# LoRA B on the halves of the array: a four-layer conditional kernel on one core

## The reference

```python
def lora_add(base, inp, A, B):
    Ab = A[layer_idx][lora_indices]
    Bb = B[layer_idx][lora_indices]
    t = jnp.einsum('bri,bni->bnr', Ab, inp)
    return base + jnp.einsum('bor,bnr->bno', Bb, t) * SCALE       # SCALE 0.5, rank 16
gate = lora_add(jnp.einsum('bnh,fh->bnf', x, W_gate), x, A_gate, B_gate)
up = lora_add(jnp.einsum('bnh,fh->bnf', x, W_up), x, A_up, B_up)  # f: 1376 columns
act = jax.nn.silu(gate) * up
down = lora_add(jnp.einsum('bnf,hf->bnh', act, W_down), act, A_down, B_down)
```

## Time and profile before

| | us |
|---|---|
| median of 3 runs | 1031.28 |
| lowest and highest | 1030.27, 1031.84 |
| the profiled execution | 1029.79 |
| its span | 1028.0 |
| TensorE busy in the span | 1001.4 |
| VectorE, GpSimd, ScalarE busy | 762.1, 486.6, 421.7 |
| from one tile's first product to the next tile's | 28.29 |

### The profile page before, as it was taken

How to read it: one execution, slowest core, us unless ns; L and a number is a source line. 1 busy time by engine, 2 the same in 40 slices (tenths; PEclk the granted TensorE clock), 3 DMA queues, 4 the chain that set the end, 5 groups by cost and what they waited for, 6 DMA issues and landing times.

```text
span 1028.0 us, 19764 instructions
## 1 busy us (share of the span) xinstructions
PE 1001.4 (97%) x5668; PEld 882.1 (86%) x5668; DVE 762.1 (74%) x2087; ACT 421.7 (41%) x660; POOL 486.6 (47%) x301
## 2 busy tenths in 40 slices
PE   2999999999999999999999999999999999999998
PEld 2666788989899899889898989998898889899987
DVE  8343387777787788777778877887777788778864
ACT  7103244344444344443444443444434444434431
POOL 0703554555544445445555444454455554454541
PEclk9999999999999999999999999999999999999999
DMA  9899543424333333435243333334352433333320
GB/s 330 309 349 336 180 114 96 140 89 131 114 112 109 105 110 102 119 95 147 81 133 112 110 109 107 105 105 121 94 146 83 132 113 108 110 107 102 112 74 21
DMA packets 101125, 135.50 MB, mean 132 GB/s; under 512 B 26411, under 2 KB 59692, under 8 KB 101100
## 3 DMA queue, kind: packets, MB, share of 16 engines
q1 hardware_dynamic: 100524, 135.12, 43.2%
q10 hardware_dynamic: 576, 0.08, 0.0%
HBM read 118.11 MB, written 16.99 MB: 131 GB/s over the span
## 4 chain that ended last, share of the span: by engine, by line
PE 91%; DMA 3%; DVE 3%; SPq 2%; issue 1%; ACT 0%; DVEq 0%; ACTq 0%
PE ps L1032 48%; PE ps L1064 27%; PE ps L1042 8%; PE ps L1010 3%; DMA x1p<-yo 1%; DMA tr<-kpad 1%; PE ps L1053 1%; PE ps L1087 1%; PE ps L1086 1%; PE ps L1023 1%; PE ps L1021 1%; PE ps L1020 1%; SPq L212 1%; SPq L279 0%; DVE xs L735 0%
## 5 line engine op out<-in xcount | busy, mean ns | idle before, releaser
L484 POOL TENSOR_TENSOR bst<-braw,bst 128x1024 fp32r<-128x1024 f32 (+1 forms) x96 | 212.8, 2217 | 313.5 <-ACT bst L591 313.5
L843 DVE STREAM_TRANSPOSE ps<-act_t 32x128 f32<-32x128 f32 x1008 | 325.3, 323 | 14.9
L1032 PE MATMUL ps<-wg_hi,x_hi 128*128 128x512 f32 (+2 forms) x768 | 292.8, 381 | 0.2 <-DVE x_lo L836 0.2
L1032 PE MATMUL ps<-wg_lo,x_hi 128*128 128x512 f32 (+2 forms) x768 | 290.2, 378 | 0.0
L1032 PE MATMUL ps<-wg_hi,x_lo 128*128 128x512 f32 (+2 forms) x768 | 289.8, 377 | 0.0
L613 ACT ACTIVATE at_hi<-ps 128x512 fp32r<-128x512 f32 (+1 forms) x95 | 53.5, 563 | 333.6 <-DVE ps L843 275.6
L843 DVE STREAM_TRANSPOSE ps<-x3m 32x128 f32<-32x128 f32 x496 | 160.0, 323 | 9.8 <-ACT x3m L558 1.2
L1032 PEld LDWEIGHTS ps<-wg_hi,x_lo 128*128 128x128 f32 x768 | 144.3, 188 | 24.9
L1032 PEld LDWEIGHTS ps<-wg_hi,x_hi 128*128 128x128 f32 x768 | 144.4, 188 | 23.0 <-issue 0.4
L1032 PEld LDWEIGHTS ps<-wg_lo,x_hi 128*128 128x128 f32 x768 | 144.4, 188 | 22.6
L1064 PE MATMUL ps<-wd_lo,at_hi 128*128 128x288 f32 x696 | 148.9, 296 | 0.0
(11 more groups left out here) (157 smaller groups left out, 1109.5 us busy)
## 6 DMA issues: line engine op xcount, KB each, us to landing
braw<-in_tb SPq DMA_DIRECT2D x256, 128.0 KB, 2.7
braw<-in_tb SPq DMA_DIRECT2D x128, 96.0 KB, 2.4
adraw<-in_tad SPq DMA_DIRECT2D x128, 88.0 KB, 1.9
tr<-kpad SPq DMA_DIRECT2D x16, 512.0 KB, 6.7
x1p<-yo SPq DMA_DIRECT2D x16, 512.0 KB, 5.1
xb<-in_x SPq DMA_DIRECT2D x32, 256.0 KB, 2.9
agraw<-in_ta SPq DMA_DIRECT2D x128, 64.0 KB, 1.9
bdraw<-in_tbd SPq DMA_DIRECT2D x128, 64.0 KB, 2.2
```

The costliest lines, as they stand in the source:

```text
L484: sub(v, b_from(p, q), v.bitcast(F32), ALU.subtract).then_inc(s["blo"], 1)
L843: last = V.transpose(to[cols].rearrange("f (k n) -> f k n", n=P)[:, :, rows], of[rows].rearrange("n (k f) -> n k f", f=P)[:, :, cols])
L1032: last = mm(bank[:, 0:n], x3s[a][:, k, :], wgs[b][:, k, o:o + n], start=(k == 0 and a + b == 0), stop=False, skip_group_check=True)
```

## The change

The two copies of a rank value no longer lie in neighbouring rows but in halves: rows 0 to 63 and rows 64 to 127, and within a half the sequence changes fastest. In gate's columns of `bst` the lower half of the rows (0 to 63) holds B's hi and the upper its lo; in up's it is the other way round (`half` takes the place of `odd`, so `b_high` is two instructions, one for gate and one for up). The products with t_hi use all 128 rows as before. The products with t_lo use only the half that holds B's hi: rows 0 to 63 for gate, rows 64 to 127 for up.

The rank values take another way: `t_pick` copies for each sequence only its own 16 values of gate and up, twice, times 0.5 (four instructions on 32 rows x 64 columns); they are turned and split at 128x64, and four DMAs issued by ScalarE (`t_scatter`) write them from SBUF to the rows and columns of `tsc` where they belong. The rest of `tsc` is zeroed once. TensorE waits for these DMAs (`tsc`) in the place of t_low.

Also, the order of the work in a tile changes on three engines. TensorE: mix comes between the two parts of chunk 0; down of the tile before moves ahead of the first lora_b; a_turn moves behind chunk 1 up and lora_b_down. VectorE: t_low ahead of a_low, x3_turn in one piece, and act_mul of chunk 0 behind td_turn, a_low of chunk 0 behind out_sum. ScalarE: x3_copy ahead of t_high, td_high ahead of ag_high, silu of chunk 1 ahead of b_high of chunk 2, ad_high ahead of x3_keep.

```diff
@@ load_b (SyncE)
-                    sp.dma_start(brs[(p + q) % 2][b * 2 * RANK:(b + 1) * 2 * RANK, 0:w],
-                                 rows.unsqueeze(1).to_broadcast([RANK, 2, w])).then_inc(s[f"b{(p + q) % 2}"], 16)
+                    sp.dma_start(brs[(p + q) % 2][b:P:GB, 0:w],
+                                 rows.unsqueeze(0).to_broadcast([2, RANK, w])).then_inc(s[f"b{(p + q) % 2}"], 16)
@@ GpSimd, once
+            pool.wait_ge(s["y"], C)
+            pool.wait_ge(s["yst0"], 16 * C // 4)
+            pool.wait_ge(s["yst1"], 16 * C // 4)
+            nc.gpsimd.memset(tsc[:].bitcast(F32), 0.0).then_inc(s["wz"], 1)
@@ b_high, t_high, t_scatter (ScalarE)
-                copy(b_view(p, q), b_from(p, q), ACT.Copy, scale=odd[:, 0:1]).then_inc(s["bhi"], 1)
+                for u in range(2):
+                    last = copy(b_view(p, q)[:, :, u], b_from(p, q)[:, :, u], ACT.Copy, scale=half[:, u:u + 1])
+                last.then_inc(s["bhi"], 1)
...
-                copy(ts2[0][:], tr2[:], ACT.Copy).then_inc(s["thi2"], 1)
+                copy(tcs[:, 0], trc[:], ACT.Copy).then_inc(s["thi2"], 1)
+
+            def t_scatter(t):
+                act.wait_ge(s["tlo2"], t + 1)
+                for b in range(GB):
+                    cols = slice(b * C, (b + 1) * C)
+                    act.dma_start(tsc[b:P:GB, :, :, cols].bitcast(F32), tcs[cols].bitcast(F32)).then_inc(s["tsc"], 16)
@@ tile_act
                 t_high(t)
-                if not last:
-                    x3_copy(t + 1)
                 b_high(t, p, 1, None if first else t * 3)
+                t_scatter(t)
                 silu(t, p, 0)
@@ VectorE
-            def t_mask(t, p):
+            def t_pick(t, p):
                 dve.wait_ge(s["la"], t + 1)
...
+                for b in range(GB):
+                    rows = slice(b * C, (b + 1) * C)
+                    of = gub[2 * (p % 2)][rows, FW[0]:FW[0] + NAG].rearrange("p (u b r) -> p u b r", u=2, b=GB)
+                    last = V.tensor_scalar(tmc[rows], of[:, :, b].unsqueeze(2).to_broadcast([C, 2, 2, RANK]), 0.5, None,
+                                           ALU.mult)
+                last.then_inc(s["tm"], 1)
@@ lora_b (TensorE)
-                    for a in range(2):
-                        last = mm(gub[2 * ((p + q) % 2) + u][:, 0:w], ts2[a][:, u, :],
-                                  bst[:, (p + q) % 2, u * n:u * n + w], start=False, stop=(a == 1),
-                                  skip_group_check=True)
+                    mm(gub[2 * ((p + q) % 2) + u][:, 0:w], tsc[:, 0, u, :], bst[:, (p + q) % 2, u * n:u * n + w],
+                       start=False, stop=False, skip_group_check=True)
+                for u in range(2):
+                    rows = slice(u * P // 2, (u + 1) * P // 2)
+                    last = mm(gub[2 * ((p + q) % 2) + u][:, 0:w], tsc[rows, 1, u, :],
+                              bst[rows, (p + q) % 2, u * n:u * n + w], start=False, stop=True, skip_group_check=True)
@@ tile_pe
                 chunk(p, 0, 0).then_inc(s["la"], 1)
+                if not last:
+                    mix(t + 1, 1 - p)
                 chunk(p, 0, 1)
-                if not last:
-                    mix(t + 1, 1 - p)
                 if not first:
                     pe.wait_ge(s["mul"], t * 3)
                 chunk(p, 1, 0)
-                pe.wait_ge(s["tlo2"], t + 1)
+                if not first:
+                    down(t - 1, 1 - p, 2)
+                pe.wait_ge(s["tsc"], (t + 1) * 16 * GB)
                 lora_b(t, p, 0)
-                if not first:
-                    down(t - 1, 1 - p, 2)
+                chunk(p, 1, 1)
+                if not first:
+                    lora_b_down(t - 1, 1 - p)
                 a_turn(t, 0)
-                chunk(p, 1, 1)
-                if not first:
-                    lora_b_down(t - 1, 1 - p)
                 lora_b(t, p, 1)
```

More of the change, by code:

```diff
@@ L114, in cond_resid_kernel @@
         wbd = sb("wbd", [P, 2, 2, P], F32R)
+        half = sb("half", [P, 2])
         wg_hi, wg_raw, wg_lo = split_buffers("wg", [P, KT, KW])
@@ L173, in cond_resid_kernel @@
         ats = [sb("at_hi", [P, T], F32R), sb("at_lo", [P, T], F32R)]
-        tm = sb("tm", [P, 2, P])
-        ts2 = [sb("t_hi", [P, 2, P], F32R), sb("t_lo", [P, 2, P], F32R)]
-        tr2 = sb("tr2", [P, 2, P])
+        tsc = sb("tsc", [P, 2, 2, P], F32R)
+        tmc = sb("tmc", [P, 2, 2, RANK])
+        trc = sb("trc", [P, 2, C])
+        tcs = sb("tcs", [P, 2, 2, C], F32R)
         tdm = sb("tdm", [P, P])
@@ L186, in cond_resid_kernel @@
             ag aghi aglo ad adhi adlo b0 b1 bhi blo bd bdhi bdlo
-            bfree la tm tmt thi2 tlo2 x3k gu silu mul att atv dn ahi alo td tdm tdt tdhi tdlo accd evac ost""".split() + [
+            bfree la tm tmt thi2 tlo2 tsc x3k gu silu mul att atv dn ahi alo td tdm tdt tdhi tdlo accd evac ost""".split() + [
             f"wl{n}" for n in range(NW)] + [f"u{q}" for q in range(C // 2)]
@@ L634, in _ @@
             x3_keep(0, 0)
+            act.wait_ge(s["wz"], 2)
             def tile_act(t, p, first=False, last=False):
@@ L642, in tile_act @@
                     a_high(t - 1, 2)
-                t_high(t)
                 if not last:
                     x3_copy(t + 1)
+                t_high(t)
                 b_high(t, p, 1, None if first else t * 3)
+                t_scatter(t)
                 silu(t, p, 0)
+                if not first:
+                    td_high(t - 1)
                 if not last:
@@ L650, in tile_act @@
                 a_high(t, 0)
-                if not first:
-                    td_high(t - 1)
+                silu(t, p, 1)
                 b_high(t, p, 2, t * 3 + 1)
-                silu(t, p, 1)
                 bd_high(t, first)
                 if not last:
+                    ad_high(t + 1, 1 - p, None if first else t)
                     x3_keep(t + 1, 1 - p, None if first else t)
-                    ad_high(t + 1, 1 - p, None if first else t)
                     b_high(t + 1, 1 - p, 0, t * 3 + 2)
@@ L817, in _ @@
             link(V.tensor_reduce(odd[:], ident.rearrange("p (n e) -> p n e", e=2)[:, :, 1:2], mybir.AxisListType.XY, ALU.add))
+            V.tensor_reduce(half[:, 0:1], ident[:, P // 2:P], mybir.AxisListType.X, ALU.add)
+            link(V.tensor_reduce(half[:, 1:2], ident[:, 0:P // 2], mybir.AxisListType.X, ALU.add))
             link(V.tensor_reduce(mask4[:], ident.rearrange("p (b e) -> p b e", b=GB), mybir.AxisListType.X, ALU.add))
@@ L923, in tile_dve @@
                     a_turn(t - 1, 2)
-                t_mask(t, p)
+                t_pick(t, p)
                 t_turn(t)
+                t_low(t)
                 if not first:
                     a_low(t - 1, 2)
-                t_low(t)
                 if not last:
-                    x3_turn(t + 1, GRID[0:8])
-                act_mul(t, p, 0)
-                if not last:
-                    x3_turn(t + 1, GRID[8:16], True)
+                    x3_turn(t + 1, GRID, True)
                 if not first:
@@ L936, in tile_dve @@
                     td_turn(t - 1)
-                a_low(t, 0)
+                act_mul(t, p, 0)
                 if not first:
@@ L940, in tile_dve @@
                     out_sum(t - 1, 1 - p, None if second else (t - 1) * 16)
+                a_low(t, 0)
                 act_mul(t, p, 1)
@@ L1105, in tile_pe @@
                 chunk(p, 0, 0).then_inc(s["la"], 1)
-                chunk(p, 0, 1)
                 if not last:
                     mix(t + 1, 1 - p)
+                chunk(p, 0, 1)
                 if not first:
@@ L1111, in tile_pe @@
                 chunk(p, 1, 0)
-                pe.wait_ge(s["tlo2"], t + 1)
-                lora_b(t, p, 0)
                 if not first:
                     down(t - 1, 1 - p, 2)
-                a_turn(t, 0)
+                pe.wait_ge(s["tsc"], (t + 1) * 16 * GB)
+                lora_b(t, p, 0)
                 chunk(p, 1, 1)
@@ L1119, in tile_pe @@
                     lora_b_down(t - 1, 1 - p)
+                a_turn(t, 0)
                 lora_b(t, p, 1)
```

8 lines of the change are left out of this document (2 added, 6 removed).

## The result

| | us |
|---|---|
| before, median of 4 runs | 1031.56 |
| after, median of 4 runs | 1320.69 (1318.66 to 1324.65) |
| ratio | 1.2805, 95% interval 1.2787 to 1.2822 |
| the profiled execution's span, before and after | 1028.0 and 1317.0 |

The forecast was 1020.5 us, with 1011 to 1047 as its range. The change is 289 us slower. First the page of the changed kernel: busy shares, the granted clock in tenths, and the DMA queues (packets, MB, share of the 16 engines' time).

A forecast was written before the change was run, and what follows sets the result against it. TensorE, busy 97% of 1028.0 us, was taken as the bound. Profiled 1029.8 - 19.9 (overlapping halves) + 7.7 (switches) + 1.7 (first tile) = 1019.3; with 1.5 for the median 1020.8, stated as 1020.5 us, range 1011 to 1047.

The forecast's parts named there:

- SyncE's loads of B: SyncE's queue: loads of B keep number and size in another row pattern, are used half a tile after b_low: free.
- Halves that run at the same time: TensorE's LoRA B: the two t_lo half products of a pair cost one pace, 0.6225 us a tile, 19.9 us less.
- The price of a switch: TensorE, whole array to halves and back in 96 groups: 0.08 us each, 7.7 in all; ends 0 and 32.6 us.
- rival B: TensorE's switches eat the gain: 1036 us at 0.12 each way, 1046 at 0.17, more if weights load late; chance 0.24.
- The transposes: TensorE's loop row taken for the switch price: entering transposes costs nothing, leaving them 0.08 us.
- the narrow products: TensorE products with 16 stationary columns, far in shape: 0.17 instead of 0.053 us before a full one, 0.12 for that switch.
- The chains around it: Other engines' work feeding TensorE: scatter, mix's x1_low and a_low stay hidden; tightest chain 8.42 us, wanted after 8.66.
- The scatter's issue: ScalarE's four transfers into tsc: 0.32 us each to issue, 2.1 to land, done at 10.2 of the tile, slack 0.9.
- First tile: First tile, once: no down covers the scatter and mix precedes x1_low, so LoRA B starts 3.0 us late; +1.7 us net.
- Rival C: TensorE's half products don't overlap: 1033 us, or 1041 with 7.7 for switches; chance 0.10.
- Rival D: The scatter into tsc lands late, at 12.4 instead of 11.1: 1.3 us a tile, 40 us, 1061; chance 0.14.
- Its mild case: Scatter with one worse value, at 11.3 or 11.2: 3 to 6 us in all, 1025; half of 0.14.

The follow-up runs named there:

- the repaired change: The changed kernel with B laid out twice in HBM by the host, so each load of B is one dimension of 32 rows: 1051.76 us, 1.0194 of before.

## Why the prediction was wrong

By its own steps:

- **SyncE's loads of B**, "the same number and size in another row pattern", were counted as free. This step failed, and it is 269 of the 289 us. Number and size were indeed the same; the number of engines was not: 2 in place of 16, and 13.64 us on the chain in place of 2.7 to landing. With 2.7 us for 128 KB there was no pressure in the profile of before that could have warned of it, only the edit itself. I gave the loads no bound.
- **Halves that run at the same time** save a pace a group: right. The pair starts together, and a second half adds 0.02 us. The run with both on one half loses 17.6 us of the 19.9 in the sum.
- **The price of a switch** was the term mis-sized: taken as 0.08 a group, with 0.34 as the upper end; measured 0.39. Entering was not free (0.10), and after the halves not one product was late but two (0.19 and 0.10). The sum with it is 1031.6 - 19.9 + 96 x 0.39 + 1.7 = 1051, and the repaired change measures 1051.8: with the loads right, this term alone still puts it outside the range. It is rival B with a price somewhat above its full one, and its clause on weights that can't be loaded under the running product is what the PEld rows show. The transposes were the wrong neighbour; the narrow products, 0.12 for one switch, were near for the way in (0.10), but showed less than the 0.29 of the way out. The rule of the Trainium skill's "TensorEngine Tiling (Array Packing)", Key Properties, that a change of mode drains the engine, was the better guide: the trace agrees with it in that every change of mode costs, 0.39 us for both ways; it doesn't show the draining itself.
- **The chains around it**: right where they could be tested, in the run with whole rows. No wait for a_low of chunk 1, the scatter behind down, mix before x1_low hidden. The scatter's issue was 0.61 to 0.65 us each, not 0.32, and still fitted: ScalarE's queue issued the first while b_high was running (615.11, in the rows below), and they landed after 1.9 (median).
- **First tile**: 1.7 us expected; 2.5 measured for it and all else that isn't a half or a load, with 0.6 to 3.9 as the interval. So the 1.7 is neither confirmed nor refuted.
- **Rival C** (no overlap) is refuted by the run with both on one half. **Rival D** (late scatter) happened, but by the loads: 8.07 us where it had 3.1 as its worst. It did name the eight loads beside the scatter, though four of them are of 96 KB and not 128. Its mild case should be 7.15 + 2.13 + 2.1 = 11.4 and not 11.3, up to 9 us and not 6; neither slip matters beside the 8.07.

ScalarE in the repaired change, for the scatter:

```profile
614.84 0.73 ACT L598 ACTIVATE bst<-braw,half 128x512 fp32r<-128x512 f32 x1
615.11 0.61 ACTq L631 DMA_DIRECT2D tsc<-tcs  x1
615.47 0.71 ACT L598 ACTIVATE bst<-braw,half 128x512 fp32r<-128x512 f32 x1
615.76 1.94 ACTq L631 DMA_DIRECT2D tsc<-tcs  x3
```

Even without the load, the change loses: what the halves save is one pace a group, 0.16 to 0.23 us, and an excursion costs 0.39. No version among these runs beats the kernel before.

## What to carry to other kernels

When a diff touches the access pattern of a DMA, write down the slowest dimension of both sides before and after; a broadcast moved to the front can take a transfer from sixteen engines to two, and the profile of before won't hint at it. Afterwards, count the packets: a difference that is a multiple of the number of DMAs shows it at once. The share of the DMA engines in a stretch with only such loads, times 16, gives the number of engines directly. Products on part of the array pay only if a run of them saves more than the 0.39 us of going there and back; here, by 0.23 or 0.16 us a pair, that would be two pairs of 512 columns or three of 352 in one go, not one. This is an estimate; no run has two pairs in a row.

## What the runs showed that I had not expected

- The scatter, on all sixteen engines, was as late as the busiest of them. Its 16 KB inside SBUF landed after 1.9 us in the median and 3.2 at most with B's loads on 16 engines, 2.4 and 6.3 with them on four, 2.4 and 8.3 on two. The median hides it: TensorE waited for it only 18 times, but up to 5.2 us.
- The slow loads also cost clock: TensorE's mean granted clock fell from 0.998 to 0.911, and its busy time is 1100.0 us against 1021.6 with good loads, for the same products. In the stretch below the granted clock is 1.00 from 619 to 626 us; TensorE then comes out of a wait of 4.32 us for the scatter, and from 629 to 631 it is 0.50, the level of 1.2 GHz. Products of 512 columns start 0.43 us apart there, not 0.23.

```profile
626.26 0.95 PE L1059 MATMUL ps<-bst,tsc 128*128 128x352 f32 x2 [4.32 <-DMA tsc<-tcs]
...
628.32 0.63 PE L1050 MATMUL ps<-wg_lo,x_hi 128*128 128x512 f32 x1
628.75 0.63 PE L1050 MATMUL ps<-wg_hi,x_lo 128*128 128x512 f32 x1
```

- With the loads on four engines the mean share of the DMA engines was only 0.36 between 600 and 700 us, and the kernel 56 us slower nonetheless: the mean over sixteen engines doesn't show that a few of them are full.
